# Fewer sampling tiles beside the preparation of one image, all the preparation of the other in one block

## The reference

```python
x = x + deform_conv_bn_relu(_gn(x))   # layer 0: offsets and masks from a 3x3 convolution
x = x + binary_1x1(_gn(x))            # layer 1
# layer 2: offsets from a 3x3 convolution, bilinear samples at 9 taps, then a 32x288 product
x = x + deform_conv(_gn(x))
# layer 3: attention over all 4096 pixels of an image
f1, f2, f3 = w1 @ g + b1, w2 @ g + b2, w3 @ g + b3      # g = _gn(x), [32, 4096]
A = softmax(f1.T @ f2, axis=-1)                         # [4096, 4096]
x = x + f3 @ A.T + g
```

## Time and profile before

| what | us |
|---|---|
| median of three runs | 1288.94 |
| profiled execution | 1288.67 |
| its span, first to last instruction | 1286.7 |
| PE busy | 1171.4 (91%) |
| VectorE (DVE) busy | 988.2 (77%) |
| ScalarE (ACT) busy | 661.2 (51%) |
| GpSimd (POOL) busy | 492.0 (38%) |
| mean granted TensorE clock | 0.949 |

### The profile page before, as it was taken

How to read it: one execution, slowest core, us unless ns; L and a number is a source line. 1 busy time by engine, 2 the same in 40 slices (tenths; PEclk the granted TensorE clock), 3 DMA queues, 4 the chain that set the end, 5 groups by cost and what they waited for, 6 DMA issues and landing times.

```text
span 1286.7 us, 20328 instructions
## 1 busy us (share of the span) xinstructions
PE 1171.4 (91%) x7126; PEld 494.0 (38%) x7126; DVE 988.2 (77%) x1679; ACT 661.2 (51%) x882; POOL 492.0 (38%) x537
## 2 busy tenths in 40 slices
PE   4999997688999999979899888988998999999996
PEld 1788884144544444423232222222222222222221
DVE  6699998875767666678788889888767777777772
ACT  4876765855555444222353453444654455554453
POOL 7000000037777777777777777774000000000000
PEclk9999998799999999955699999999999999999998
DMA  2655550058454441111121111111000000000000
GB/s 54 143 130 115 114 115 1 1 168 235 125 175 135 142 126 54 51 46 51 52 53 50 51 51 51 51 51 33 1 1 1 1 17 1 0 0 0 0 1 16
DMA packets 59672, 79.21 MB, mean 62 GB/s; under 512 B 12230, under 2 KB 43974, under 8 KB 59414
## 3 DMA queue, kind: packets, MB, share of 16 engines
q1 hardware_dynamic: 44342, 47.03, 14.1%
q0 software_dynamic: 15264, 31.29, 8.7%
HBM read 70.94 MB, written 7.34 MB: 61 GB/s over the span
## 4 chain that ended last, share of the span: by engine, by line
PE 49%; POOL 19%; DVE 14%; issue 11%; ACT 4%; SPq 1%; DMA 1%; DVEq 1%; POOLq 0%; ACTq 0%
POOL tile_data L554 19%; PE psum L1971 13%; PE psum L1953 9%; PE psum L1994 8%; PE psum L1718 6%; DVE maxes L1144 4%; PE psum L1733 3%; DVE probs_and_weighted L881 3%; PE psum L1668 2%; PE psum L1745 2%; PE psum L2000 2%; DVE probs_and_weighted L891 1%; PE psum L1916 1%; ACT quads L1574 1%; PE psum L1736 1%
## 5 line engine op out<-in xcount | busy, mean ns | idle before, releaser
L554 POOL DMA_INDIRECT tile_data<-quad_table,index_u x477 | 468.2, 982 | 390.2 <-DMA quad_table<-quad_rows_or_splits 245.1
L1144 DVE TENSOR_REDUCE maxes<-psum 128x1 f32<-128x512 f32 x512 | 326.0, 681 | 93.9 <-PE psum L1953 92.3
L1574 ACT ACTIVATE quads<-psum 128x1024 f32<-128x1024 f32 x256 | 248.1, 1021 | 248.6 <-PE psum L2000 248.6
L1971 PE MATMUL psum<-quads 128*64 128x512 f32 x1024 | 256.8, 610 | 0.0
L1833 PE MATMUL psum<-scratch,quad_rows_or_splits 128*128 128x512 f32 (+1 forms) x486 | 210.7, 574 | 5.9 <-DVE scratch L966 5.9
L1994 PE MATMUL psum<-quads,probs_and_weighted 32*128 32x512 f32 x1024 | 147.9, 647 | 2.2 <-ACT quads L1574 1.5
L1833 PEld LDWEIGHTS psum<-scratch,quad_rows_or_splits 128*128 128x128 f32 x486 | 88.3, 193 | 103.0 <-issue 87.6
L1953 PE MATMUL psum<-products_or_attention 128*128 128x512 bf16 x256 | 91.3, 419 | 36.2 <-DVE maxes L1144 36.2
L978 DVE TENSOR_TENSOR probs_and_weighted<-psum,quads 128x512 f32<-128x512 f32 (+1 forms) x81 | 51.2, 642 | 73.6 <-PE psum L1833 68.3
L1971 PEld LDWEIGHTS psum<-quads 128*64 128x64 f32 x1024 | 58.8, 136 | 120.4 <-issue 111.3
L1433 ACT ACTIVATE vals<-psum 96x384 f32<-96x384 f32 x53 | 25.8, 486 | 142.7 <-PE psum L1797 142.7
(11 more groups left out here) (227 smaller groups left out, 1400.8 us busy)
## 6 DMA issues: line engine op xcount, KB each, us to landing
products_or_attention<-positions SPq DMA_DIRECT2D x30, 576.0 KB, 8.1
products_or_attention<-bands SPq DMA_DIRECT2D x12, 768.0 KB, 7.5
tile_data<-quad_table,index_u POOLq DMA_INDIRECT x477
quads<-bands SPq DMA_DIRECT2D x6, 768.0 KB, 10.5
quad_table<-quad_rows_or_splits SPq DMA_DIRECT2D x4, 768.0 KB, 8.4
products_or_attention<-bands SPq DMA_DIRECT2D x4, 576.0 KB, 6.7
quad_table<-quad_rows_or_splits SPq DMA_DIRECT2D x2, 640.0 KB, 8.4
products_or_attention<-positions SPq DMA_DIRECT2D x4, 288.0 KB, 7.5
```

Source lines behind the costliest of these rows:

```text
L554: pool.indirect_dma_start(out=out[:, k * CORNERS * C:(k + 1) * CORNERS * C], out_offset=None, in_=table, in_offset=bass.IndirectOffsetOnAx ...
L1144: v.reduce_max(maxes[:, tile_of_q, block_of_k:block_of_k + 1], psum[:, FREE + c % 2, :], AXIS_X)\
L1574: act.activation(probs[:, s % 2, 2 * BLK * h:2 * BLK * (h + 1)], psum[:, SCORES + 2 * h:SCORES + 2 * h + 2, :].rearrange("p a n -> p (a n) ...
L1971: last = pe.matmul(psum[2 * C * h:2 * C * h + 2 * C, SUMS, :], f3[b][:, 4 * s + i, :], probs[:, s % 2, BLK * i:BLK * i + BLK], start=s == ...
```

## The change

- `FIRST_MERGED` is 2: four tiles of image 1 lie beside the preparation of image 0, the other 28 in seven merged blocks (0 to 6).
- The preparation of image 0 goes by the eight key blocks k, not by tiles. Before each group of four chunks comes one fill (five before the first group); a turn of a tile and a packed fill lie between chunks two and three of a group (`TURNED_BETWEEN`, `PACKED_BETWEEN`), a convolution ahead of a group. The first chunk of group k waits until fill k + 1 has been read by VectorE, as before. VectorE has tile 2 behind group 2 and tile 3 behind group 4, ahead of the reads of the next fill.
- The six packed or turned fills have their own semaphores, go to bank `SUMS` (image 0) or `SAMPLES` (image 1), and are copied by ScalarE, not VectorE.
- The normalised image 0 is written in two halves; that of image 1 in four quarters by VectorE, not ScalarE.
- All the preparation of image 1 lies in block 7: normalisation in quads 0 and 1, nine fills in quads 1 to 3 (over three banks), the 32 chunks in quads 4 to 6 as 11, 11 and 10, the six packed fills in quads 4 to 7.
- The last query fill of the preparation of image 1 waits for ScalarE's copy of the last packed fill.

```diff
-FIRST_MERGED = 4
+FIRST_MERGED = 2
-LAST_SCORED = [0, 0, 6, 7, 7, 7, 5, 0]
+LAST_SCORED = [0, 0, 0, 0, 11, 11, 10, 0]
-FIRST_FILLS = 16
-FILLS_BESIDE = [[0, 1, 2], [3, 4], [5, 6], [7, 8], [9, 10], [11, 12], [13, 14, 15], []]
-SCORED_BESIDE = [0, 4, 4, 6, 6, 6, 6, 0]
+FIRST_FILLS = NBLK + 2
+PACKED = 6
+FILLS_BEFORE = [[0, 1, 2, 3, 4], [5], [6], [7], [8], [9], [], []]
+PACKED_BETWEEN = [None, 0, 1, None, 2, 3, 4, 5]
+TURNED_BETWEEN = {0: 1, 3: 2, 6: 3}
+CONVOLVED_BEFORE = {1: 1, 4: 2, 7: 3}
+FILLED_IN = {(1, 2): [0, 1], (2, 0): [2], (2, 1): [3], (2, 2): [4], (3, 0): [5], (3, 1): [6], (3, 2): [7, 8]}
+PACKED_IN = {(4, 0): 0, (4, 2): 1, (5, 1): 2, (6, 0): 3, (6, 2): 4, (7, 1): 5}
```

VectorE, preparation of image 0:

```diff
+            for k in range(NBLK):
+                read_fill(0, k + 1)
+                largest(0, first, range(4 * k, 4 * k + 4), keys_first=True)
+                if k == 2:
+                    finish(1, pair_of(0), 1)
+                if k in (2, 4):
+                    weight_corners(1, pair_of(1), k // 4, copied=False)
+                    sum_corners(1, pair_of(1), k // 4)
+                if k == 5:
+                    finish(1, pair_of(1), 0)
```

VectorE, normalisation of image 1 in block 7:

```diff
+                    for k in range(4):
+                        quarter = slice(N // 4 * k, N // 4 * (k + 1))
+                        v.tensor_scalar(g2[0:C, quarter], x_of[1][:, quarter], norm[rows, n, 0:1], norm[rows, n, 1:2],
+                                        ALU.mult, ALU.add).then_inc(g3_ready, 1)
```

ScalarE, copies of the packed fills:

```diff
+            def take_packed(b, i):
+                kind, at = "pprrvv"[i], i % 2
+                bank = psum[:, packed_bank(b), :]
+                act.wait_ge(packed, PACKED * b + i + 1)
+                if kind == "p":
+                    act.activation(keys[b][:, BLK * at:BLK * at + BLK], bank, ACT.Identity).then_inc(moved, 1)
```

TensorE, preparation of image 0:

```diff
+            for k in range(NBLK):
+                if k in CONVOLVED_BEFORE:
+                    t = CONVOLVED_BEFORE[k]
+                    convolve(1, pair_of(t // 2), t % 2)
+                for n in FILLS_BEFORE[k]:
+                    fill(0, n)
+                score_chunks(0, first, range(4 * k, 4 * k + 2), keys_first=True)
+                if k in TURNED_BETWEEN:
+                    t = TURNED_BETWEEN[k]
+                    turn(1, pair_of(t // 2), t % 2)
+                if PACKED_BETWEEN[k] is not None:
+                    fill_packed(0, PACKED_BETWEEN[k])
+                score_chunks(0, first, range(4 * k + 2, 4 * k + 4), keys_first=True)
```

TensorE, preparation of image 1, at three places in a quad of block 7:

```diff
+            def prepare_image_1(s, place):
+                for n in FILLED_IN.get((s, place), ()):
+                    fill(1, n)
+                if (s, place) in PACKED_IN:
+                    fill_packed(1, PACKED_IN[s, place])
```

More of the change, by code:

```diff
@@ L330, in fill_bank, with packed_bank @@
                 return SAMPLES if b else FREE + 1
[L331 to L338, removed]
+            return (SAMPLES, FREE, FREE + 1)[n % 3] if b else SCORES + n % 4
+        def packed_bank(b):
+            return SAMPLES if b else SUMS
         PARTS_BANK, ADDED_BANK, TURNED_BANK = 3, 4, 4
@@ L1084, in l3_normed @@
                 v.tensor_scalar(one_more[rows, :], norm[rows, n, 0:1], 1.0, None, ALU.add)
-                v.tensor_scalar(g2[0:C, :], x_of[0], norm[rows, n, 0:1], norm[rows, n, 1:2], ALU.mult, ALU.add)\
-                    .then_inc(g3_ready, 1)
+                for h in range(2):
+                    here = slice(N // 2 * h, N // 2 * (h + 1))
+                    v.tensor_scalar(g2[0:C, here], x_of[0][:, here], norm[rows, n, 0:1], norm[rows, n, 1:2],
+                                    ALU.mult, ALU.add).then_inc(g3_ready, 1)
             def read_fill(b, n, block=None):
@@ L1095, in read_fill, with prepare_image_1 @@
                 fills = n if isinstance(n, tuple) else (0, 0, n + FILLS * b)
[L1096 to L1115, removed]
+                v.wait_ge(high_taken, lin(fills, 1, 1))
+                if n == 0 and b == 0:
+                    v.wait_ge(rest_cols, 1)
+                dst = (qa if kind == "q" else ka)[b][:, here]
+                c = 0 if kind == "q" else 1
+                v.scalar_tensor_tensor(dst, dst, keep_rest[:, c:c + 1], psum[:, fill_bank(b, n), :], ALU.mult, ALU.add)\
+                    .then_inc(fill_read, 1)
+            def prepare_image_1(s):
                 n, rows = NORM_3 + 1, IMAGE[1]
-                if (j, s) == (NBLK - 2, 0):
-                    step(v.memset(f3[1][:, :, C:2 * C], 1.0))
+                if s == 0:
                     v.wait_ge(finished_stat, 2 * NBLK)
                     v.bn_aggr(mv[rows, n, 0:2], stats[rows, 0:NBLK, :]).then_inc(var_ready, 1)
-                if (j, s) == (NBLK - 2, 1):
+                    step(v.memset(f3[1][:, :, C:2 * C], 1.0))
+                if s == 1:
                     v.wait_ge(dev_ready, n + 1)
@@ L1514, in take_fill @@
                 kind, at = ("q", None) if block is not None else fill_kind(n)
-                if kind not in "qk":
-                    return
                 if block is None:
@@ L1591, in attention @@
                     attend(b, (0, 0, 0), first=True, tiles=True, ahead=True)
-                    with act.Fori(1, MERGED) as j:
+                    with act.Fori(1, MERGED - 1) as j:
                         attend(b, (j, 1, 0), tiles=True, ahead=True)
-                    for j in range(MERGED, NBLK):
-                        attend(b, (0, 0, j), last=j == NBLK - 1, prepare=lambda s, j=j: prepare_image_1(j, s))
+                    attend(b, (0, 0, MERGED - 1), tiles=True)
+                    attend(b, (0, 0, NBLK - 1), last=True, prepare=prepare_image_1)
                 else:
@@ L2023, in attend @@
                         score_chunks(b_next, nxt, range(cuts[1 + half], cuts[2 + half]))
+                        if prepare is not None:
+                            prepare(s, 1 + half)
                     c += m
```

182 lines of the change are left out of this document (89 added, 93 removed).

## The result

| | median us | runs | ratio to before, 95% interval |
|---|---|---|---|
| before | 1289.58 | 4 | |
| after | 1307.07 (1302.23 to 1314.23) | 4 | 1.014 [1.0084, 1.0195] |

A forecast was written before the change was run, and what follows sets the result against it. PE was taken to set the blocks, and PE at half clock plus waits the preparation; -6.0 + 0 + 1.1 + 12.6 + 0.6 = +8.3 on 1288.67 gave 1297 us, range 1292 to 1302, down to 1288 with B and part of A.

The forecast's parts named there:

- Preparation of image 0: Stage beside image 1's first sampling tiles: four tiles fewer, new waits for fill reads, 72.6 to 66.6 us, 6.0 less.
- Rival A: Half clock ends inside the preparation, at about 570; total 1285, faster; chance 0.16 (0.10 faster, 0.06 around no change).
- my signs of being wrong: The prediction is wrong if the clock returns before 582 in the preparation, or block 7 stays under 50 us.
- my single price, half clock throughout: Preparation priced with PE at 1.2 GHz all through, the clock returning 11 to 15 us after its end.
- Blocks 0 to 6: Block 0 and the five merged blocks unchanged; block 6 becomes a merged block, 46.4 instead of 45.3 us, 1.1 more.
- Block 7: Block holding all of image 1's preparation: 45.6 to 58.2 us, 12.6 more, bounds 51.0 and 63.
- PE's pieces at full clock: Block 7's quads summed from full-clock times, such as scores 1.29, a fill 1.05, a packed fill 0.99 us.
- rival C: Half clock returns in quads 0 and 1 of block 7; three quads cost 12 to 15 us, total 1311; chance 0.05.
- The rule that I named beside rival A: The Trainium skill has activity release TensorE's throttle, making rival A the likely case; the profile rows were held against it.
- First block of image 1: Its last query fill waits 1.4 us for ScalarE's copy of the last packed fill: 0.6 more, between 0 and 1.5.
- Rival B: Block 7 costs only PE's work, 51.0 us, chunks not waiting for reductions; total 1290, no change; chance 0.09.
- Table load: Block 7: the skill's drain of about 1.38 us per table switch, some 2.8 us for two, was not added.

The follow-up runs named there:

- the unaltered kernel: The changed kernel run again with no edit, as a baseline: 1307.25 us, ratio 1.012 to before.
- the kernel with the first gap alone: The changed kernel with one added 128x128x512 multiplication at the end of quad 0 of block 7, none ahead of fill 0: 1302.8 us.
- the early reads: The changed kernel with VectorE's reads of the fills in the preparation put one group earlier: 1299.26 us, ratio 1.0079 to before.
- the two other fillings: Early reads and three multiplications ahead of fill 0, plus three ahead of image 1's first-block fill and five ahead of tile 2's turn: 1288.46 us, ratio 0.9979.
- the kernel before with late chunks: The kernel before with image 1's 32 chunks in quads 4 to 6 as 11, 11, 10, instead of quads 2 to 6: 1293.72 us, ratio 1.003.

## Why the prediction was wrong

The direction was right, the size was not: 1297.0 forecast, 1307.07 measured, outside of 1288 to 1302.

- **Preparation of image 0**: right in its mechanism. The waits were forecast at 3.1, 2.7, 2.1 and 0.3 and measured at 2.85, 2.24, 2.11 and 0.19, no wait of VectorE for a gather is left. The stage came out 1.8 us shorter than the sum, 0.8 of them in the waits. The clock returned at 612.8, 3.3 us ahead of the mark, where I had 11 to 15 behind it, and fell again for 6.8 us in block 0. Rival A, a return before 582, did not happen in this execution. But it is one of my signs of being wrong, and it came in the unaltered kernel's second profile: the clock was back at 569 for 7 us, then at half again, and the stage was 4 us shorter. Eight profiles hold this same preparation; in five of them the clock came back for some 7 us at 567 to 569, and the stage, counted as in the table, took 57.9 to 65.0 us at 37.5 to 61 us of half clock. That is 0.3 us of length for each us at half on the whole, as in my rival. So the stage has a spread of its own that my single price, half clock throughout, could not hold; that assumption failed in the direction of faster.
- **Blocks 0 to 6**: right, within half a microsecond each (-0.5, 0, +0.6 against 0, 0, +1.1).
- **Block 7**: the step that failed and that the forecast hung on. "PE's pieces at full clock" was taken for all eight quads. The waits were sized correctly (0.21 and 0.93 against 0.3 and 0.9), the four quads at full clock came out within 0.15 us, and with the clock held up the block measured 57.6 us against my 58.2. But quads 2, 3 and most of 4 ran at half: 15.2 us. That is rival C, with its cause only half named and its place a little early (I had quads 0 and 1, the clock fell at the start of quad 2), at a price of 12 to 15 us which was about right, and to which I gave 5%. Against it I put "my waits there are 0.3 and 0.9 us", as if idle time were the only thing to weigh. What I passed over is what the quads hold. Every quad has scores of 32 rows and subtractions of 3; the change adds nine fills of 33 rows to quads 1 to 3 and takes the chunks of 128 rows out of quads 2 and 3, so that only the weighings read 128 rows there. The experiments show both parts: three multiplications of 128 rows in the wait ahead of fill 0 keep the clock up, the same of 33 rows do not.
- The rule that I named beside rival A bears on this one too. TensorE had work in flight 33.4 of 34.1 us and stayed at 1.2 GHz. The Trainium skill, "TensorE: Matmul & The Clock Gate", section "What's actually happening", says that activity releases the throttle, and its section "HAM oscillation — how this bites in real kernels" has the fall follow a long wait for data. The trace disagrees if activity is taken as the busy share of the profile: the fall came behind 0.93 us of idle time, and in the kernel with 33-row fillings behind almost none. What the chip takes for activity these runs do not show, beyond the difference between added work of 33 and of 128 rows.
- The row that could have warned me is in the earlier trace rows: in the preparation PE was busy 60.5 of 72.6 us at a mean clock of 0.52. I used this against rival A and not for rival C. The stage's largest group is twenty fills of 33 rows, with transposes and packed fills.
- **First block of image 1**: forecast +0.6, measured +3.5. At full clock (the kernel with the first gap alone) it is 40.0, so +1.2; the other 2.3 are again a half clock, behind a wait of 1.27 us for which I had 1.4. Behind the same wait the clock fell in some profiles and not in two others, so the wait alone does not decide it.
- **Rival B**, no waits for reductions: wrong, PE waited 0.57 and 0.21 us in front of single chunks throughout quads 4 to 6, for instance:

```profile
987.62 0.39 PE L1973 MATMUL psum<-quad_rows_or_splits,tile_data 128*128 128x512 bf16 x1 [0.57 <-DVE maxes L1133]
988.22 0.39 PE L1973 MATMUL psum<-quad_rows_or_splits,tile_data 128*128 128x512 bf16 x1 [0.21 <-DVE maxes L1133]
```

- **Not in the forecast**: 2.7 us in the part before the preparation, with a stretch at half clock of 6.8 us in place of 3.4 there. The change does not touch that part, and the second profile of after has 3.4. At twice the time for the same work the longer stretch accounts for at most 1.7 us; over all kept profiles this part ends between 547.4 and 551.3, so it has a spread of its own.
- **Table load**: the exponentials start 0.01 us behind it (0.02 before), as said:

```profile
946.78 1.28 ACT L1575 ACT_TABLE_LOAD   x1
948.07 1.94 ACT L1575 ACTIVATE quads<-psum 128x1024 f32<-128x1024 f32 x2
```

What the change gains in the preparation, 7.8 us in this profile, is smaller than the 12.0 us that its block 7 costs at full clock. With three multiplications added the change still loses, by a little (1.0026 [1.0007, 1.0044]): in that profile the preparation was 12.0 us shorter than before and block 7 12.0 longer, and the first block of image 1, with a half clock in it, 3.8 longer. It wins, by 0.2%, only with the early reads and the two other fillings.

## What to carry to other kernels

When an edit gathers small matmuls into one stretch and moves the large ones out, price the stretch at both clocks, and ask what rows its matmuls read, not only how long TensorE idles. If the profile shows the clock falling where the engine seems busy, three spare full-height matmuls in the last wait ahead of it are a cheap test of the cause, and perhaps the cure. A stage whose length follows the clock has to be compared between profiles with the same time at half clock, or an edit is credited with what the clock did. Chunks that trade two banks with a reducing engine should be spread over as many quads as can hide the reductions.

## What the runs showed of the hardware

- Fillings of 0.82 us of 128-row matmuls in the wait ahead of fill 0 kept the clock at 2.4 GHz over the whole block in two profiles (57.6 and 57.5 us) and for all but 3.4 us in a third (58.6). With fillings in both waits, 128 rows gave 3.4 us at half (59.1), 33 rows for the same time 34.1 (72.7).
- The half clock lasted 34.1 us with TensorE in flight for 33.4 of them, and 6.8 us, and 3.4 more later, when fourteen matmuls of 128 rows were put between the fills.
- More work made the kernel faster: 18 added matmuls took 11 us from the block, and 8.6 from the median.
- The place of the fall is stable in block 7 (in all five profiles in which nothing of 128 rows was added directly ahead of fill 0 or between the fills, the stretch lasted 34.1 or 34.2 us). It is not in the preparation, where the same program had its clock at half for 61, 58, 48 or 37.5 us, nor at the start of image 1's first block.
- The short falls stand without an explanation: in four profiles, the kernel before with late chunks among them, the clock fell for 3.4 to 6.8 us behind the eleven chunks of quad 4, in others of the same block it did not.
